# Cross attention and self attention: second value projection between the groups of the cross weighted sum, last key transpose behind it

## What is computed

```python
q = (query @ Wq + bq); k = (key_in @ Wk + bk); v = (key_in @ Wv + bv)     # split into 16 heads
scores = jnp.einsum('bhqd,bhkd->bhqk', q, k) / jnp.sqrt(jnp.float32(hd))
scores = ALPHA * (scores * mask) + (1.0 - ALPHA) * scores
attn = jax.nn.softmax(jnp.clip(scores, -50.0, 50.0), axis=-1)
context = jnp.einsum('bhqk,bhkd->bhqd', attn, v)
resid = query + context @ Wo + bo                                          # then a layer norm
```

```python
xn = rms_norm(x, attn_norm_w)
q, k, v = jnp.split(xn @ to_qkv_w, 3, axis=-1)
q, k = (rope(q), rope(k))
scores = jnp.einsum('bhid,bhjd->bhij', q, kf) * DH ** (-0.5)
probs = jax.nn.softmax(jnp.where(mask[None, None], scores, -1e+30), axis=-1)
o = jnp.einsum('bhij,bhjd->bhid', probs, vf)                               # to_out_w, then ff_w1, silu gate, ff_w2
```

## Time and profile before

| | us |
|---|---|
| median of 3 runs | 1765.45 |
| lowest, highest | 1764.08, 1776.49 |
| profiled execution | 1785.61 |
| its span, first to last instruction | 1783.8 |
| mean granted TensorE clock of the span | 0.934 |
| TensorE busy | 1629.0 (91%) |
| VectorE busy | 1200.8 (67%) |
| ScalarE, GpSimd busy | 799.2, 795.1 (45%) |

### The profile page before, as it was taken

The page is one execution under the profiler, slowest core; times in us unless marked ns, Lnnn a source line. Parts: engine busy times, 40 slices in busy tenths (PEclk is TensorE's granted clock), DMA queues, the critical chain, the costliest instruction groups (busy, mean ns, idle before and its releaser), DMA issues.

```text
span 1783.8 us, 59422 instructions
## 1 busy us (share of the span) xinstructions
PE 1629.0 (91%) x22051; PEld 1361.4 (76%) x22051; DVE 1200.8 (67%) x3215; ACT 799.2 (45%) x1933; POOL 795.1 (45%) x1105
## 2 busy tenths in 40 slices
PE   2899999999999999999999999999999999999997
PEld 1677878877778777877877877878877777877876
DVE  2576766676766667677676766676676667667674
ACT  1344444444444544444444444444444544444453
POOL 2254454354453454454354444354454454353452
PEclk9898998999988989899898999998999989899899
DMA  6000000000000000000000000000000000000000
GB/s 166 15 20 14 14 19 14 14 19 14 14 19 12 16 14 19 14 19 14 14 19 14 15 18 14 14 19 12 15 19 12 15 14 18 14 14 17 16 14 5
DMA packets 52891, 33.92 MB, mean 19 GB/s; under 512 B 12214, under 2 KB 51659, under 8 KB 52747
## 3 DMA queue, kind: packets, MB, share of 16 engines
q1 hardware_dynamic: 52874, 33.70, 7.1%
HBM read 20.82 MB, written 4.46 MB: 14 GB/s over the span
## 4 chain that ended last, share of the span: by engine, by line
PE 47%; DVE 13%; issue 11%; SPq 8%; DMA 7%; ACT 6%; POOL 6%; DVEq 1%; POOLq 0%; ACTq 0%
PE psum L861 12%; SPq L376 7%; DMA q_heads<-q_parts 7%; PE psum L818 6%; PE psum L934 5%; ACT vall L476 4%; POOL z L423 4%; PE psum L835 3%; PE psum L882 3%; DVE z L640 3%; DVE o L656 2%; ACT qT L476 2%; PE psum L976 2%; PE psum L866 2%; PE psum L844 2%
## 5 line engine op out<-in xcount | busy, mean ns | idle before, releaser
L416 POOL TENSOR_TENSOR ra<-ra,rb 128x512 f32<-128x512 f32 x256 | 322.2, 1279 | 8.3
L640 DVE TENSOR_TENSOR z<-psum,wT 77x512 f32<-77x512 f32 x256 | 164.5, 682 | 143.2 <-PE psum L818 142.9
L631 DVE TENSOR_TENSOR ra<-psum,rope 128x512 f32<-128x512 f32 x256 | 175.1, 684 | 82.8 <-PE psum L810 77.7
L861 PE MATMUL psum<-qT,kall 64*81 64x64 f32 x4096 | 228.0, 276 | 0.4 <-DVE mx L714 0.4
L861 PEld LDWEIGHTS psum<-qT,kall 64*81 64x81 f32 x4096 | 208.0, 188 | 16.6 <-issue 3.1
L427 POOL TENSOR_TENSOR st<-st,nhalf 128x1 f32<-128x1 f32 x64 | 35.0, 548 | 413.4 <-DVE st L682 413.4
L423 POOL TENSOR_SCALAR z<-z 77x512 f32<-77x512 f32 x256 | 153.5, 610 | 136.5 <-DVE z L640 136.5
L818 PE MATMUL psum<-q_heads,k_parts 32*77 32x512 f32 x768 | 120.1, 416 | 85.1 <-DMA q_heads<-q_parts 83.6
L577 ACT ACTIVATE probs<-psum 81x512 f32<-81x512 f32 x256 | 131.3, 594 | 146.8 <-PE psum L866 146.8
L468 POOL TENSOR_TENSOR st<-st,nhalf 128x1 f32<-128x1 f32 x64 | 37.5, 586 | 351.3 <-DVE st L736 351.3
L523 ACT ACTIVATE z<-z 77x512 f32<-77x512 f32 x256 | 153.5, 640 | 69.3 <-POOL z L423 69.3
(11 more groups left out here) (130 smaller groups left out, 3298.8 us busy)
## 6 DMA issues: line engine op xcount, KB each, us to landing
seq_in<-in SPq DMA_DIRECT2D x64, 166.5 KB
q_heads<-q_parts SPq DMA_DIRECT2D x256, 32.0 KB, 1.8
out<-out_sb SPq DMA_DIRECT2D x64, 64.0 KB, 1.6
maskT<-in SPq DMA_DIRECT2D x64, 38.5 KB
vall<-memv_dram SPq DMA_DIRECT2D x128, 4.0 KB, 1.9
ctx_all<-in SPq DMA_DIRECT2D x5, 320.0 KB, 12.6
wqkv<-in SPq DMA_DIRECT2D x1, 1536.0 KB, 9.9
ctx_all<-in SPq DMA_DIRECT2D x3, 288.0 KB, 11.2
```

The costliest lines, as they stand in the source:

```text
L416: nc.gpsimd.tensor_tensor(ra[:, sl], ra[:, sl], rb[:, sl], ALU.add).then_inc(rot_ready, 1)
L631: V.tensor_tensor(ra[:, sl].rearrange("n (h d) -> n h d", h=8), p, rope[:, 0, :].unsqueeze(1).broadcast_to([S, 8, DH]), ALU.mult)
L640: V.tensor_tensor(z0[:, 4 * t:4 * t + 4, :], cross_at(f"score{t}")[0:S2, :].rearrange("k (h q) -> k h q", h=4), wT[:].unsqueeze(1).broadca ...
L861: mm(self_at(f"score{t}")[0:KEYS, S * n + SEG * s:S * n + SEG * (s + 1)], kall[dims, 4 * half + n, s, :], qT[dims, 4 * half + n, SEG * s:S ...
```

## The change

On TensorE alone the order of four blocks in a body is changed. Before: q1 transposes, v1 projection, k1 transposes, weighted sum of groups 0 to 3. After: q1 transposes, groups 0 and 1, v1 projection, groups 2 and 3, k1 transposes. The wait for the weighted sum's bank moves ahead with group 0, and each group keeps its wait for its exponential. The banks, the semaphores' counts and the other engines' lists are as before.

```diff
                 if a is not None:
                     turn("q1")
+                if c is not None:
+                    wait(pe, cross_free("pv", c))
+                    pe.wait_ge(exp0_ready, c * 4 + 1)
+                    weigh_cross(0)
+                    pe.wait_ge(exp0_ready, c * 4 + 2)
+                    weigh_cross(1)
+                if a is not None:
                     project("v1")
+                if c is not None:
+                    pe.wait_ge(exp0_ready, c * 4 + 3)
+                    weigh_cross(2)
+                    pe.wait_ge(exp0_ready, c * 4 + 4)
+                    weigh_cross(3).then_inc(cross_fill("pv"), 1)
+                if a is not None:
                     turn("k1")
-                if c is not None:
-                    wait(pe, cross_free("pv", c))
-                    for g in range(4):
-                        pe.wait_ge(exp0_ready, c * 4 + (g + 1))
-                        last = weigh_cross(g)
-                    last.then_inc(cross_fill("pv"), 1)
                 if a is not None:
```

More of the change, by code:

```diff
@@ L942, in body @@
                     turn("q1")
-                    project("v1")
-                    turn("k1")
                 if c is not None:
                     wait(pe, cross_free("pv", c))
-                    for g in range(4):
-                        pe.wait_ge(exp0_ready, c * 4 + (g + 1))
-                        last = weigh_cross(g)
-                    last.then_inc(cross_fill("pv"), 1)
+                    pe.wait_ge(exp0_ready, c * 4 + 1)
[3 more added lines that the diff above has]
+                if a is not None:
+                    project("v1")
+                if c is not None:
[4 more added lines that the diff above has]
+                if a is not None:
+                    turn("k1")
                 if a is not None:
```

## The result

| | before | after |
|---|---|---|
| median of the runs, us | 1769.76 (4 runs, 1764.08 to 1776.49) | 1983.79 (4 runs, 1980.9 to 1990.29) |
| profiled execution, time and span, us | 1785.61, 1783.8 | 1985.25, 1983.5 |
| mean granted TensorE clock | 0.934 | 0.868 |

The kernel after takes 1.1213 of the time before, 95% interval 1.1157 to 1.1269: 12% slower, on the forecast of 1981 us. (Ratios here leave out executions over 1.5% above the fastest of the same kernel, so one can differ from the quotient of two medians, most of all in e7.)

A forecast was written before the change was run, and what follows sets the result against it. The prediction took TensorE's order and length in the changed stretch as the bound. Removed waits worth 0, 88 us for later maxima and 128 us for clock falls, added to the 1765.45 us median, gave 1981 us; range 1845 to 2029.

The forecast's parts named there:

- the clock: Half-clock stretches (falls) during or just after the maxima go from 24 to all 62 bodies, 3.36 us each: +128 us.
- the stall: Maxima start 1.4 us later in each of 63 bodies, from bank wait and exposed k1 copy: +88 us.
- The start of the sum: Groups 0 and 1 wait for VectorE's first multiply to release their PSUM bank, starting at 901.38.
- The hole for the copy of kall: Between k1 transposes and maxima, TensorE idles 0.83 us for VectorE's copy, formerly hidden by the weighted sum.
- From the maxima to the shift: Stays 2.97 to 2.99 us: the 0.22 us cover isn't won, since row maxima are late next.
- The wait rows: TensorE should idle some 0.8 us before L844 in 63 bodies, where the row named ACT vall.
- The mean clock of 0.83: Sign of the forecast: TensorE's mean clock for the core near 0.83, nearly every body at 0.83 to 0.88.
- rival 3: Projection amid the weighted sum stops every fall, giving back 80.7 us; 1737 us, or 1773 with 1.4 us stall; chance 0.10.
- Rival 1: Falls stay as they are; only the exposed copy and bank wait count, +88 us, 1854 us; chance 0.18.
- Rival 2: Falls in about two thirds of the bodies, 16 more than before, 54 us, 1907 us; chance 0.22.

The follow-up runs named there:

- e7: Kernel before with eight unused 9-column matmuls between the two halves of the maxima, where TensorE idled 0.22 us; 1798.48 us, ratio 1.0069 to before.
- e1: Kernel before with only the k1 transposes moved behind the whole weighted sum, v1 projection still in front; 1993.5 us, ratio 1.1208 to before.
- e2: Kernel before with only the v1 projection moved between groups 1 and 2, k1 transposes still before the sum; 1751.24 us, ratio 0.9855 to before.
- e4: Kernel after with 24 unused 9-column matmuls filling the hole between k1 transposes and maxima; 1967.9 us, ratio 1.1077 to before.
- e6: Kernel before with one unused 512-column matmul between the two halves of the maxima, where TensorE idled 0.22 us; 1740.63 us, ratio 0.9840 to before.
- e3: Kernel after with three unused 512-column matmuls filling the hole between k1 transposes and maxima; 1819.3 us, ratio 1.0242 to before.
- e5: Kernel after with the k1 transposes put back in front of groups 2 and 3, behind the v1 projection; 1741.36 us, ratio 0.9854 to before.
- e9: Kernel after with the first of three v1 projection matmuls moved in front of group 0, into the bank wait; 2011.47 us, ratio 1.1352 to before.
- e10: e5 with the first of three v1 projection matmuls moved in front of group 0, into the bank wait; 1736.24 us, ratio 0.9793 to before.
- e11: The kernel of e5 run again on another chip, beside e10; 1741.37 us, ratio 0.9825 to before.

## Why the prediction was right

The time, 1983.8 us, lies 3 us from the forecast. That closeness is in part luck. Terms were off in opposite ways: the clock was put 31 us too high, the stall 9 us too low, and 7 us of the first body weren't in the sum. What is left over, 16 us too many (216 for the 199.7 between the two profiled executions), doesn't show in the forecast of the median, because the profiled execution before was itself 16 us over its median. For the profiled execution my sum gave 2002 us, and it took 1985.25.

**Right as put.** The bound was TensorE's order in this stretch. Nothing that the change removes was worth anything: no exponential was waited for, before or after. The start of the sum waits for VectorE's first multiply (predicted 901.38, measured 901.37 in the same frame), the projection follows at 902.41 (902.36) and groups 2 and 3 at 903.30 (903.24). The hole for the copy of kall is 0.83 us, just as read off the last body of the kernel before. From the maxima to the shift it takes 2.96 us (2.97 to 2.99), and for the reason given: the second half of the maxima now comes 0.60 us after the first where it took 0.78, so the wait for vall is gone, but the self scores (L861) then wait for VectorE's row maxima (1040.63, 0.30 us) and start 1.65 us after the start of the maxima, where it was 1.67. The wait rows changed as said: 60 times 0.8 us before L844, vall gone. One reading was off, and nothing rests on it: the copy ends 0.10 us before the maxima start, in the last body of the kernel before and in the kernel after, not 0.07. e1 and e2 show that the hole comes of the k1 move alone.

**The stall, the term mis-sized by a tenth.** Taken as 1.4 us, measured 1.56 (bounds 0.83 to 1.6), so 97 us in 62 bodies for 88 in 63. The hole was right. Missing were some 0.05 us at each of the two switches from the weighted sum to the block behind it (1034.53 to 1035.57 and 1036.46 to 1037.49 are 1.04 and 1.03 us, where I took 0.98), which I had listed as a possible cost and not taken, and 0.06 us more for the transposes behind a thin block (0.66 us, not 0.60).

**The clock, number and price.** I took a fall in all 62 bodies at the old mean price, +128 us. Measured: 47 falls, 3.77 us each, +96.5 us. The mean clock of 0.83 that I had named as a sign didn't come either: it is 0.868. The number was too high, since the projection in the middle of the sum does help (e2: 8 falls, against 24 before), which I had put down as rival 3 and given too little weight beside the hole: e1, without that help, has 61. The price was too low: nearly all falls are now of the long kind that cost 3.92 us before. The reason given, a longer thin stretch that ends in a true hole, holds in half. The thin work counts; the hole counts nearly like thin work, and it isn't needed as idle time (e4).

**Not priced.** The first body took 7.3 us more. Over the kernels of this study it took 34.3 to 46.4 us in no relation to their order, e6 being one of the longest and one of the fastest, so I don't put it to the change. Why it varies stays open.

**The rivals.** Rival 1, falls unchanged at 1854 us, had the stall alone right: e3, which has the same stall and few falls left, takes 1819 us. Rival 2 was nearer in the number of falls than my forecast (40 for the 47 measured, where I took 62), at the old price and the smaller stall, hence 1907. Rival 3 is e5 in all but the copy: break the stretch and hide the copy, and the clock never falls. By the page TensorE: Matmul & The Clock Gate of the Trainium skill, section A second HAM failure mode: psum-queue depth-cycling, short idling between groups of matmuls made the clock swing in another kernel. The runs agree only in that it swings with no long gap; e4, in which that idling is filled, swings on.

**Left open.** Why 47 and not 62: bodies fall three in four, e9's all do, and e1's all but one. The table gives the direction in which dense work moves the number of falls, and no rule that would have given 47, or 0 for e5. In e2, e5, e9 and e10 the length of the body changes along with the order, and no run holds one of them fixed; only e3 and e4 have the length of the kernel after.

## What to carry to other kernels

Before a block is moved behind the work that follows it, look at what that work was hiding: here 1.97 us of thin matmuls hid a 0.69 us copy, and a place in the same trace where the cover is missing (the last body) gave the hole to the hundredth. Cut a long loop into one window a body and read the granted clock of each: the busy share stood at 90% while the clock cost 177 us. Where a tuned loop has falls of the clock, put its dense blocks amid its narrow ones, keep each copy beside the other half, and try it on the chip, since each such order moved the time by some per cent and in the direction only partly foreseen.

## What the runs showed of the hardware

- TensorE's busy time doesn't keep its clock. In the hole of the kernel after (47 falls of 3.77 us), 0.94 us of 512-column matmuls left 12 falls of 1.23 us and 0.87 us of 9-column ones 43 of 3.73. In that of the kernel before (24 falls), one dense matmul left 8 falls and eight thin ones 32.
- Work that nobody uses can pay: e6 issues 64 more matmuls (22115 for 22051) and is 1.6% faster.
- The place counts: the same dense matmul some 6 us earlier than the last key transposes left the falls as they were (21 for 24).
- A longer body can be a faster kernel: e5's bodies take 0.55 us more than those of before at full clock, none falls, and it gains 1.5 to 1.8%.
- The spread between runs of one kernel follows the clock. The four of the kernel after have spans of 1979.1, 1980.6, 1983.5 and 1988.5 us at mean clocks of 0.872, 0.869, 0.868 and 0.865; e5's four runs, at 0.991 to 0.994, stay within 0.2 us. The same kernel in e11 spreads over 11 us, from 1733.66 us at 0.999 to 1744.87 at 0.989, with no fall in the bodies of its profiled execution: that execution's first body took 41.5 us at 0.75.
